# Per-sample weights with a residual: where three bias tiles are made, in which order the plan's steps stand, and when GpSimd begins its loads

## The reference

```python
def ref(x, cat_ids, W, b):
    selected_W = W[cat_ids]                 # [128, 256, 256]
    selected_b = b[cat_ids]                 # [128, 256]
    return x + jnp.einsum('bsd,bdh->bsh', x, selected_W) + selected_b[:, None, :]
# x [128, 64, 256] float32, cat_ids int32 in 0..63, W [64, 256, 256], b [64, 256]
```

## Time and profile before

| | us |
|---|---|
| median of 3 runs | 106.52 (105.53 to 107.8) |
| the profiled execution's own time | 107.0 |
| its span in the profile | 105.3 |
| busy in the span: TensorE | 90.7 |
| ScalarE | 56.3 |
| VectorE | 56.2 |
| GpSimd | 45.8 |

### The profile page before, as it was taken

How to read it: one execution, slowest core, us unless ns; L and a number is a source line. 1 busy time by engine, 2 the same in 40 slices (tenths; PEclk the granted TensorE clock), 3 DMA queues, 4 the chain that set the end, 5 groups by cost and what they waited for, 6 DMA issues and landing times.

```text
span 105.3 us, 3045 instructions
## 1 busy us (share of the span) xinstructions
PE 90.7 (86%) x786; PEld 60.5 (57%) x786; DVE 56.2 (53%) x137; ACT 56.3 (53%) x99; POOL 45.8 (43%) x81
## 2 busy tenths in 40 slices
PE   0039999999958838999999999999999999999960
PEld 0026576656626517557576767666766767676630
DVE  1086403558848696175547473829282828364740
ACT  0000866556324618279766666667585858584400
POOL 5000078977888889867678353005503011000000
PEclk9999999999999998599999999999999999999999
DMA  0576998999999999999999999926883805999994
GB/s 10 150 266 170 345 340 274 356 325 339 377 396 351 389 402 361 353 401 387 364 363 398 406 361 375 403 90 120 254 332 120 280 11 184 330 343 326 305 344 168
DMA packets 18049, 31.26 MB, mean 297 GB/s; under 512 B 1840, under 2 KB 13296, under 8 KB 18032
## 3 DMA queue, kind: packets, MB, share of 16 engines
q0 software_dynamic: 5696, 19.40, 51.5%
q1 hardware_dynamic: 10816, 10.36, 29.3%
q10 hardware_dynamic: 1520, 1.31, 4.4%
HBM read 25.30 MB, written 8.39 MB: 320 GB/s over the span
## 4 chain that ended last, share of the span: by engine, by line
PE 59%; DMA 14%; issue 11%; POOLq 4%; POOL 4%; DVE 3%; ACT 1%; SPq 1%; ACTq 0%
PE mm_ps L522 39%; PE xt_ps L436 11%; DMA w_all<-in_L_cond_W 10%; PE mm_ps L508 6%; DMA cat_col_i<-in_itok_B 4%; POOL w_all L159 3%; POOLq L153 2%; POOLq L159 2%; PE xt_ps L522 2%; POOL rows L168 1%; ACT w_slot L281 1%; DVE rows L405 0%; DVE same_ahead L354 0%; SPq L153 0%; DVE in_category L364 0%
## 5 line engine op out<-in xcount | busy, mean ns | idle before, releaser
L522 PE MATMUL mm_ps<-w_slot,xT 128*64 128x256 f32 x496 | 58.5, 385 | 4.0 <-ACT w_slot L281 3.9
L281 ACT COPY w_slot<-w_all 128x512 f32 x64 | 39.0, 620 | 31.4 <-SPq L204 16.5
L522 PEld LDWEIGHTS mm_ps<-w_slot,xT 128*64 128x64 f32 x496 | 35.4, 140 | 22.0 <-issue 6.2
L159 POOL DMA_DIRECT2D w_all<-in_L_cond_W x56 | 33.2, 595 | 14.8 <-issue 7.3
L405 DVE TENSOR_TENSOR rows<-mm_ps,rows 128x512 f32<-128x512 f32 (+1 forms) x32 | 21.5, 673 | 25.3 <-PE mm_ps L522 24.5
L281 DVE COPY w_slot<-w_all 128x512 f32 x64 | 26.7, 446 | 13.4 <-SPq L204 13.3
L168 POOL DMA_DIRECT2D rows<-in_x x14 | 10.9, 781 | 26.4 <-DMA out<-rows 16.1
L436 PE MATMUL xt_ps<-ident,rows 128*128 128x128 f32 x128 | 19.9, 304 | 0.1
L436 PEld LDWEIGHTS xt_ps<-ident,rows 128*128 128x128 f32 x128 | 15.6, 154 | 7.0 <-issue 6.0
L293 ACT COPY xT<-xt_ps 128x512 f32<-128x512 f32 x32 | 17.1, 584 | 0.0
L508 PE MATMUL mm_ps<-bias_parts,is_sample 96*64 96x256 bf16 x124 | 10.8, 297 | 0.0
(11 more groups left out here) (42 smaller groups left out, 13.1 us busy)
## 6 DMA issues: line engine op xcount, KB each, us to landing
w_all<-in_L_cond_W POOLq DMA_DIRECT2D x56, 256.0 KB
out<-rows SPq DMA_DIRECT2D x30, 256.0 KB, 4.1
rows<-in_x POOLq DMA_DIRECT2D x14, 512.0 KB, 7.6
rows<-in_x SPq DMA_DIRECT2D x2, 512.0 KB, 4.6
w_all<-in_L_cond_W ACTq DMA_DIRECT2D x4, 256.0 KB, 4.8
w_all<-in_L_cond_W SPq DMA_DIRECT2D x4, 256.0 KB, 6.1
out<-rows SPq DMA_DIRECT2D x2, 128.0 KB, 2.9
out<-rows ACTq DMA_DIRECT2D x2, 128.0 KB, 2.9
```

The source lines that it names most:

```text
L159: engine.dma_start(w_all[:, n, :, :], weights[bass.ds(c, 1), :, :].rearrange("c (k p) h -> p (c k) h", p=P), **how).then_inc(first_w_loade ...
L281: copy(w_slot[:, PAIR * p + half, :, :].rearrange("p k h -> p (k h)"), w_all[:, bass.ds(c, 1), :, :].rearrange("p c k h -> p (c k h)")).th ...
L522: last = T.matmul(to[HALF * half:HALF * (half + 1), :], xT[:, slot, k, j, :], w_slot[:, j, k, :], start=False, stop=(k == K - 1), skip_gro ...
```

## The change

There are three edits. First, the three later bias tiles are no longer made at the start and copied by ScalarE. Tile `g` is made in group `g` (1 to 3), behind the transposes for the next group, straight into a PSUM bank that is used only in the next group (banks 0, 2 and 0 in turn), and VectorE splits it from there. Second, on VectorE the steps that only `slot_words` and the bias need (`same`, `place_powers`, `in_category`) move behind the copy that makes `load_words`. Third, GpSimd waits for five reports where it waited for three, and reads its first word of the list before that wait.

```diff
-REPORTED_FIRST = 3
+REPORTED_FIRST = 5
-PLAN_STEPS = {"samples": 6, "first": 9, "bias": 13, "list": 14, "slots": 16}
+PLAN_STEPS = {"samples": 6, "first": 9, "list": 12, "slots": 15, "bias": 16}
-        bias_of = sb("bias_of", [ROWS, TILES - 1, H])
-        bias_ps = [mm_ps[r][0:ROWS, n, :] for r, n in ((2, 0), (1, 1), (3, 0), (3, 1))]
+        bias_ps = [mm_ps[r % BANKS][0:ROWS, 0, :] for r in (2, 4, 6, 8)]
...
             pool.wait_ge(plan_read, 1)
+            word = words_read(mybir.EngineType.Pool, load_words[0:1, FIRST_LOADS // WORD:FIRST_LOADS // WORD + 1],
+                              2 ** (WORD * BITS) - 1)[0]
             pool.wait_ge(w_loads_done, REPORTED_FIRST)
             load_rows(pool, FIRST_X)
             for n in range(FIRST_LOADS, C):
-                if n % WORD == 0:
+                if n % WORD == 0 and n > FIRST_LOADS:
...
-            act.wait_ge(plan_products, 5)
-            nc.scalar.copy(bias_of[:, 0, :], bias_ps[1]).then_inc(bias_copied, 1)
-            nc.scalar.copy(bias_of[:, 1:TILES - 1, :], mm_ps[3][0:ROWS, :, :]).then_inc(bias_copied, 1)
...
             for g in range(GROUPS - 1):
+                if 1 <= g < TILES:
+                    dve.wait_ge(tiles_made, g)
+                    dve.wait_ge(bias_ready, PAIR * g)
+                    split_bias(g, bias_ps[g])
...
-                if g + 1 < TILES:
-                    dve.wait_ge(bias_copied, 2)
-                    dve.wait_ge(bias_ready, PAIR * (g + 1))
-                    split_bias(g + 1, bias_of[:, g, :])
...
+            pe.wait_ge(plan_step, PLAN_STEPS["bias"])
             pe.wait_ge(bias_loaded, 16)
             bias_of_tile(0).then_inc(plan_products, 1)
...
-            pe.wait_ge(plan_read, 1)
-            for t in range(1, TILES):
-                last = bias_of_tile(t)
-            last.then_inc(plan_products, 1)
...
                 pe.wait_ge(xT_ready, K * (g + 1))
+                if 1 <= g < TILES:
+                    pe.wait_ge(sums_added, QUADS_IN_GROUP * (g - 1) + 1)
+                    bias_of_tile(g).then_inc(tiles_made, 1)
                 if g == 0:
                     pe.wait_ge(bias_ready, PAIR)
-                    pe.wait_ge(bias_copied, 2)
-                if PAIRS_IN_GROUP * g % PAIRS_IN_TILE == 0:
-                    pe.wait_ge(bias_ready, PAIR * (PAIRS_IN_GROUP * g // PAIRS_IN_TILE + 1))
+                elif 1 < g <= TILES:
+                    pe.wait_ge(bias_ready, PAIR * g)
```

More of the change, by code:

```diff
@@ L132, in build_cond_residual @@
         plan_read = sem("plan_read")
-        bias_copied = sem("bias_copied")
+        tiles_made = sem("tiles_made")
         bias_step = sem("bias_step")
@@ L361, in _ @@
             V.tensor_scalar(cat_powers[:, :], powers[:, :], cat_col[:, 0:1], None, ALU.mult).then_inc(plan_step, 1)
-            V.tensor_scalar(same[:, :], cat_row_i[:, :], cat_col[:, 0:1], None, ALU.is_equal).then_inc(plan_step, 1)
+            steps[0] += 2
             dve.wait_ge(consts_ready, 5)
-            V.tensor_scalar(in_category[:, :, :, :], cat_row_i[0:C, :].rearrange("c (t n) -> c t n", n=TILE)
-                            .unsqueeze(2).broadcast_to([C, TILES, SPLITS, TILE]),
-                            iota_part[0:C, 0:1], None, ALU.is_equal).then_inc(plan_step, 1)
-            steps[0] += 4
-            assert steps[0] == PLAN_STEPS["bias"]
             dve.wait_ge(plan_products, 1)
@@ L374, in _ @@
             step(V.tensor_scalar(place[:, :], place_ps, FAR, first_here[:, 0:1], ALU.add, ALU.mult))
-            step(V.tensor_scalar(place_powers[:, :], powers[:, :], place[:, 0:1], None, ALU.mult))
-            assert steps[0] == PLAN_STEPS["slots"]
             dve.wait_ge(plan_products, 2)
             V.tensor_copy(load_words[:, :], mm_ps[1][0:1, 0, 0:LIST_WORDS + 1]).then_inc(plan_read, 1)
+            V.tensor_scalar(same[:, :], cat_row_i[:, :], cat_col[:, 0:1], None, ALU.is_equal).then_inc(plan_step, 1)
+            V.tensor_scalar(place_powers[:, :], powers[:, :], place[:, 0:1], None, ALU.mult).then_inc(plan_step, 1)
+            steps[0] += 2
+            assert steps[0] == PLAN_STEPS["slots"]
+            V.tensor_scalar(in_category[:, :, :, :], cat_row_i[0:C, :].rearrange("c (t n) -> c t n", n=TILE)
+                            .unsqueeze(2).broadcast_to([C, TILES, SPLITS, TILE]),
+                            iota_part[0:C, 0:1], None, ALU.is_equal).then_inc(plan_step, 1)
+            steps[0] += 1
+            assert steps[0] == PLAN_STEPS["bias"]
             dve.wait_ge(plan_products, 3)
```

## The result

The changed kernel takes 107.91 us (median, 107.43 to 109.08), the kernel before 106.41 beside it. The ratio is 1.012, with a 95% interval of 1.0065 to 1.018, so the change makes the kernel slower by about 1.3 us. The profiled execution took 108.12 us, with a span of 106.4.

A forecast was written before the change was run, and what follows sets the result against it. Loads set the pace up to about 40 us, TensorE behind it. Idle DMA engines 1.85 us, less 0.55 for the earlier start, less 0.6 coming back, gave 0.7: 106.52 + 0.7 = 107.2 us, range 105.5 to 108.7.

The forecast's parts named there:

- its own list: Prediction wrong if group 3's last pair starts ahead of 39.3 or behind 41.9, or half clock lies outside group 4.
- the pair: Last pair of group 3 on TensorE, at 39.77 in the kernel before, predicted to start at about 40.5.
- the sum: Delay of the loads from GpSimd's start: 1.85 - 0.55 - 0.6 = 0.7 us later, bounds -0.5 and 2.15.
- the hole: DMA engines stand still until GpSimd's first packets at 15.9 to 17.8: 0.9 to 2.8 us, 1.85 in the middle.
- the weak stretches: DMA rates below 363 GB/s at 13, 16 and 17 us, lacking 0.83 us, of which 0.6 was to come back.
- The start: List of loads made earlier on VectorE, so everything starts 0.55 us earlier (0.4 to 0.6).
- Nothing catches up: Behind GpSimd's late start the DMA engines are full, so no delay is made good; no size given.
- one to one: The kernel's end follows the landing of loads in the list's order, by the same amount.
- No hole: Rival at GpSimd's start: report 5 comes early, only the 0.55 us of the earlier list remain, 106.0; chance 0.24.
- TensorE's chain counts: Rival in early group 0: up to the tiles' 2.87 us less 0.5 come out, 104.2; chance 0.05.
- The full delay: Rival at GpSimd's start: report 5 at 15.1, all its transfers 2.15 us later, 108.7; chance 0.08.
- The clock: Rival on TensorE: a fall to 1.2 GHz in group 5 or later adds an unhidden 1.6 us, 108.8; chance 0.13.

The follow-up runs named there:

- e3: The kernel before with the third edit alone (GpSimd waits for five reports, first word read ahead of the wait): 108.39 us, ratio 1.022.
- e2: The kernel before with the first edit alone (later bias tiles made in groups 1 to 3): 106.31 us, ratio 1.000.
- e4: The kernel before with the second edit alone (list of loads made ahead of the plan's other steps on VectorE): 106.60 us, ratio 1.000.
- e10: The changed kernel with GpSimd beginning only at the eighth report: 108.62 us, ratio 1.022 against the kernel before.
- e1: The changed kernel with GpSimd beginning at three reports again, the word still read ahead: 104.82 us, ratio 0.988 against the kernel before.
- e5: The kernel before with only the first word of the list read ahead of GpSimd's wait, three reports kept: 105.44 us, ratio 0.991.
- e6: The changed kernel with GpSimd beginning at the first report instead of the fifth: 104.95 us, ratio 0.9865 against the kernel before.
- e12: The changed kernel, five reports kept, with group 2's rows issued by SyncE and the words for loads 8 to 27 read ahead of GpSimd's wait: 106.85 us.
- e8: The changed kernel with three reports and the first word read behind the rows of group 2: 106.23 us, ratio 0.993 against the kernel before.

## Why the prediction was right or wrong

**Held.** The start of GpSimd decides (e3 has all of the loss, e2 and e4 none). The rows of group 2 went out at 15.22 and load 8 at 16.11, inside 13.9 to 15.8 and 14.8 to 16.7. The fifth report came at 14.9, between 13.2 and 15.1. The list came 0.4 earlier, for 0.55. The bias tiles took 0.67 each and cost nothing. TensorE waited ahead of the transposes of group 2. The half clock stood in group 4 again, but a second time in group 1 as well, which by its own list counts against the prediction. 107.91 is inside the range and 0.7 above the forecast, and the pair came at 41.65, where I had said 40.5, just inside the 41.9 at which I would have called the prediction wrong. Some of it is luck. The first packets of GpSimd's queue came at 16.8, where the middle of the sum has 14.85 + 2.0, but by terms that cancel: the fifth report was at 14.91 and not in the middle at 14.15, the rows went out 0.31 us behind it and not 0.69, and the first packet came 1.6 us behind them and not 2.0. And by the traces 0.8 us of the delay came back at the end, by the stores, of which the sum says nothing.

**The sum was mis-sized.** It said 1.85 for the hole, less 0.55, less 0.6 for the weak stretches, 0.7 in all, and the pair came 1.88 later. In the terms of the sum:
- The start brought 0.41 and not 0.55.
- The 0.6 of the weak stretches did not come back, and this is the largest error. From 12 to 20 us the engines moved less than before: (337 - 262) x 4 and (307 - 242) x 4 GB/s are 0.56 MB, which is 1.5 us at 363 GB/s. The copy at 28.64 was 1.42 us late, and 1.85 - 0.41 is 1.44: the hole had its size, and nothing was made good in it.
- "Nothing catches up" held, but another 0.46 us was lost between the copy at 28.64 and the pair at 41.65. It isn't that GpSimd's queue moved less, since it had 2.99 MB from 20 to 30 us in both kernels. What these 0.46 us are stays open.
- Why the gap between reports 3 and 5 was so long the rows didn't tell, and I had the traffic of GpSimd under suspicion. The changed kernel had a gap of 3.0 us without any such traffic, and e10 one of 1.8. So such a gap doesn't take GpSimd's traffic, and it is longer than two loads at the full rate (1.4 us): in the changed kernel the last parts of load 3 came late.
- That the end follows the landing of loads "one to one" left out the stores. In the profiled executions 0.8 of the 1.88 came back behind the last sum. By the traces of the other kernels this belongs to the one execution of the kernel before at least as much as to the change, and the medians (1.5 apart) lie between.

**Rivals.** "No hole" is refuted by the 55 GB/s, and "TensorE's chain counts" by e2. "The full delay" had 2.15 us for load 8, and it was 1.57. "The clock": there was one fall more than before, in group 1, put where TensorE waits for copies anyway, and the fall in group 4 was hidden for the most part, as I had worked out. Of the 17 executions of the kernel before in e1's ratio, nine had a mean clock of 0.996 or more, with 106.1 us on average, and eight 0.984 or a little under, with 106.4; the other three sets have 0.3 to 0.4 us between such groups. By this a fall goes with 0.3 to 0.4 us, where I had 0.5. The rule of the Trainium skill (TensorE: Matmul & The Clock Gate, Why this matters for your kernels) is against long idle gaps between bursts. Here the clock fell at 42.75 with no wait of TensorE since 9 us longer than the 1.91 ahead of the pair at 41.65, and at 25.69 behind waits of 1.25 and 0.74 us, while in e1 the same pair waited 1.86 us and no fall followed. So the length of the longest wait doesn't tell by itself when a fall comes.

**The price of a transfer.** The rows of group 2 landed 4.0 us after their issue in the changed kernel, where it was 5.9. The estimate of 3.2 us by the Trainium skill (DMA: Bandwidth & Descriptors, Anatomy of one DMA) is nearer to this, though still 0.8 short. TensorE waited 0.20 us for this transfer, in front of transposes that stood 0.9 earlier than before.

**What was in the change.** The two halves of the third edit pull against each other: reading the word ahead brings 0.9% (e5), and the two more reports cost about 3 us, both with the other edits (the changed kernel against e1, 3.1) and without them (e3 against e5, 3.0). The best of these kernels are e1 and e6 with 104.82 and 104.95, 1.2 to 1.35% under the kernel before and 2.4 (by the ratios) to 2.9% (by the medians) under the changed one.

## What to carry to other kernels

When one engine's transfers take over from those of other queues, what counts is whether its first packets are there when the others run dry. From issue to first packet it was 1.6 us in the changed kernel, so a start that waits for the others' transfers to be reported comes too late, and in none of these kernels was all of the time made good in which the engines stood still. Stretches in which they look less than full in the profile of before are no reserve to count on. Filling the gap from another queue brought nothing that can be told from the noise here. Count the start of an engine in reports, but read in the trace how far apart these are, since they need not be even. And an engine that will wait anyway should read what it needs ahead of the wait, not behind it.

## What was not expected of the hardware

- GpSimd's start at the first, third, fifth and eighth report gave medians of 104.95, 104.82, 107.91 and 108.62: a step of 3.1 us between three and five, 0.7 behind it and none ahead. The starts themselves are unevenly spaced (the rows of group 2 at 11.67, 12.82, 15.22 and 16.73), and ahead of 15 us GpSimd's queue moved next to nothing in e1 and e6.
- The engines' share and their rate part ways: 0.96 with 289 GB/s in e12, 1.03 with 347 GB/s in e6, both in the same stretch of 19 to 27 us.
- A single one of the 16 parts of a load can be late by far: in the kernel before, 15 parts of load 3 were there at 13.45 us and the last at 15.37, and every report behind it had to wait.
- The third report scatters by more than the 0.4 us by which the list was moved: with the list early it came at 11.90, 11.95, 12.51 and 12.78 (the changed kernel, e8, e1, e4), with the list late at 11.99, 12.22, 12.32 and 12.48 (e5, e3, the kernel before, e2).
